# ScalarE's order in graph attention: the copy of the transposed probabilities ahead of the leaky ReLU in every slot

## The chip, the cores and the metric

The kernel runs on one core of one Trainium2 chip. The metric is the time of one execution on the device in microseconds (us), as a median over runs.

## What is computed

`x` holds 16 graphs of 1024 nodes with 256 features; `adj` holds their 1024 x 1024 adjacency matrices. One layer is graph attention with a residual, then a mixture of eight experts with a residual. The attention part, in which the change lies:

```python
h = _layernorm(x)
Wh = einsum('bnd,od->bno', h, W)
e = (Wh @ a1)[:, :, None] + (Wh @ a2)[:, None, :]
e = where(e > 0, e, 0.2 * e)          # leaky ReLU
e = where(adj == 0, -inf, e)
alpha = softmax(e, axis=-1)
x = x + einsum('bij,bjo->bio', alpha, Wh)
```

The second part applies to each row of the layer-normalised result, for each of eight experts, two matrix products with batch norm and ReLU and a third product, and adds them with weights of a softmax gate.

## The kernel before

The program has two blocks, one after the other: attention (to about 684 us) and the experts. Each engine has an instruction stream of its own, written out in a fixed order; engines meet through semaphores. The change is in ScalarE's stream of the attention block.

A batch (graph) is eight row tiles of 128 nodes. The block is a software pipeline of slots, one tile per slot: 16 slots `u` make a pair `k` of batches, and there are 8 pairs, with six slots ahead (`u` from -6). A tile `t` passes through several slots, at an offset from `u`:

- `t = u + 6`, VectorE: adjacency row and the row of the second score term give `scores` (L973).
- `t = u + 5`, ScalarE: `relu`, the leaky ReLU (Prelu) of the masked scores, in place (L789).
- `t = u + 4`, VectorE: `row_min` (L946), then ScalarE: `exponentials`, in place, with the row sum (L808). It signals `probs_ready`.
- `t = u + 3`, TensorE: 8 transposes `pT_ps<-ident,scores` (L681), which wait for `probs_ready`; ScalarE: `upper_half`, which copies `pT_ps` from PSUM to `pT_hi` in a shortened format (L799) and waits for those transposes (`pT_ready`); VectorE: the remainder `pT_lo` (L983).
- `t = u + 2`, TensorE: 24 matmuls `attn_ps` (L53 to L55), in the three products of upper and lower halves.
- `t = u + 1`, VectorE: normalise and add the residual (L956); ScalarE: negated mean (L839, every second slot) and sum of squares (L850).

So the tile that a slot's exponential finishes is the one that the next slot's transposes and copy take. TensorE's order in a slot is transposes, then any projection, then the 24 matmuls.

In four of the eight slots of a batch TensorE also projects the next batch's rows (call it head work; in the code `head and 1 <= head[1] <= HEADS`): four transposes of x (L638) at the end of the slot before, the projection (L655), ScalarE's copies `hT` (L757) and `wh_hi` (L766), VectorE's `wh_lo` (L925). The slot behind these four, with `head[1] == HEADS + 1`, opens on TensorE with eight transposes that spread a column over rows (L664), which ScalarE copies (`ej_rows`, L772); call it the row slot. In it, and in slot 10 of the last pair, the exponential stands ahead of the squares (`exp_first`). The row slot and the three behind it have no head work. The last batch has none in any slot, since no batch follows.

Of the kernel before, what the change touches and what calls it, by code (L numbers as in the profile page):

```python
# [282 lines left out]
def attention_block(nc, x, adj, W, a, W1, W2, x1_dram, ident, minus_half, ln_eps, w12_hi, w12_lo, feat_sum,  # L283
# [11 lines left out]
    HEADS = TB // 2  # L295
# [11 lines left out]
    with ctx:  # L307
# [65 lines left out]
        def tile_at(k, u, off, last):  # L373

            t = u + off
            ok = (t >= 0 or not isinstance(k, int)) and (t < UT or not last)
            return ok, t, k * UT + (t + 1)
# [18 lines left out]
        def task_at(k, i):  # L396

            return i // EP, k * EP + i % EP
# [21 lines left out]
        def parity(t):  # L420
            return (t // TB) % 2
# [330 lines left out]
        @block.scalar  # L752
        def _(act):
            def head_hT(b, j, first=False):
                xT, hT_j, _ = (first_head if first else later_head)(j)
                act.wait_ge(S["hT_psum"], b * HEADS + (j + 1))
                act.activation(hT_j.rearrange("p k c -> p (k c)"), xT, ACT.Copy) \  # L757
                    .then_inc(S["hT_ready"], 1)

            def head_wh(b, j, i, first=False):  # L760
                _, _, acc = (first_head if first else later_head)(j)
                act.wait_ge(S["xs_rstd_ready"], b * HEADS + (j + 1))
                for c in range(2):
                    t = 2 * j + c
                    act.wait_ge(S["wh_ready"], b * TB + (t + 1))
                    act.activation(wh_hi[i][:, t, :], acc[:, 1 - c, 0:D], ACT.Copy,  # L766
                                   scale=xs_rstd[:, j, 1 - c:2 - c]).then_inc(S["wh_hi_ready"], 1)

            def head_ej(b, i):
                act.wait_ge(S["ej_rows_psum"], 2 * b + 1)  # L770
                rows = (head_ps if b else attn_ps)[:, 0, :]
                act.activation(ej_rows[i][:, 0:BANK], rows, ACT.Copy, scale=-EDGE_UNIT) \  # L772
                    .then_inc(S["ej_left_ready"], 1)

            def split_weights_hi(k, i):

                layer, e = task_at(k, i)
                act.wait_ge(stage_in[i % 2], DMA * (k * EP + (i // 2 + 1)))
                act.activation(w12_hi[:, layer, e, :], w_stage[i % 2][:, :], ACT.Copy).then_inc(S["w12_hi_ready"], 1)

            def relu(k, u, last):

                ok, t, n = tile_at(k, u, 5, last)
                if ok:

                    act.wait_ge(S["masked_ready"], n)
                    if k == 0 and t < TB:
                        act.wait_ge(S["wh_lo_ready"], t // 2 * 2 + 2)
                    act.activation(scores[t % 4][:, 0:N], scores[t % 4][:, 0:N], ACT.Prelu, scale=SLOPE / EDGE_UNIT,  # L789
                                   bias=e_cols[parity(t)][:, (t % TB) ^ 1, 0:1], alpha=1.0 / SLOPE) \  # L790
                        .then_inc(S["lrelu_ready"], 1)

            def upper_half(k, u, last):

                ok, t, n = tile_at(k, u, 3, last)
                if ok:
                    act.wait_ge(S["pT_ready"], n)
                    wait(act, S["attn_ready"], n - 2)
                    act.activation(pT_hi[t % 2][:, :, :], pT_ps[t % 2][:, :, :], ACT.Copy) \  # L799
                        .then_inc(S["pT_hi_ready"], 1)  # L800

            def exponentials(k, u, last):

                ok, t, n = tile_at(k, u, 4, last)
                if ok:
                    c = slice(t % 4, t % 4 + 1)
                    act.wait_ge(S["min_ready"], n)
                    act.activation(scores[t % 4][:, 0:N], scores[t % 4][:, 0:N], ACT.Exp, scale=-1.0,  # L808
                                   bias=row_min[:, c], accum_out=row_sum[:, c]).then_inc(S["probs_ready"], 1)

            def slot(k, u, last):
                head = head_at(k, u, last)
                if head and 1 <= head[1] <= HEADS:
                    head_hT(2 * k + head[0], head[1] - 1)
                if head and head[1] == HEADS + 1:
                    head_ej(2 * k + head[0], head[0] % 2)
                if head and 1 <= head[1] <= HEADS:

                    upper_half(k, u, last)
                    relu(k, u, last)  # L820
                else:
                    relu(k, u, last)
                    upper_half(k, u, last)
                if head and 1 <= head[1] <= HEADS:
                    head_wh(2 * k + head[0], head[1] - 1, head[0] % 2)

                if last and u == GATE_SLOT + 2:
                    for d in range(KB):
                        act.wait_ge(first_tile.xT_psum, d + 1)
                        act.activation(first_tile.xT_hi[:, d, :], head_ps[:, d, :], ACT.Copy) \  # L830
                            .then_inc(first_tile.xT_hi_ready, 1)
                exp_first = (head and head[1] == HEADS + 1) or (last and u == NORM_SLOT + 1)
                if exp_first:
                    exponentials(k, u, last)

                post, pt, pn, pc = pair_at(k, u, 1, last)
                if post:
                    act.wait_ge(S["x1_ready"], k * UT + (pt + 1))
                    act.activation(x1_negmean[:, pc], x1_sum[:, pc], ACT.Copy, scale=-1.0 / D) \  # L839
                        .then_inc(S["x1_negmean_ready"], 1)  # L840
                squares = [pair_at(k, u, 1, last) + (-1,), pair_at(k, u, 0, last) + (0,)]
                if last and u == UT - 2:
                    squares[1] = pair_at(k, u + 1, 0, last) + (0,)
                if last and u == UT - 1:
                    squares = []
                for post, pt, pn, _, step in squares:
                    if post:
                        at = (pt + step) % 4
                        act.wait_ge(S["x1_negmean_ready"], pn)
                        act.activation(w_sb[:, at % 2, :], x1_sb[at][:, :], ACT.Square, bias=x1_negmean[:, at:at + 1],  # L850
                                       accum_out=x1_squares[:, at:at + 1]).then_inc(S["x1_squares_ready"], 1)
                if not exp_first:
                    exponentials(k, u, last)
                if u >= 0 and u % TASK_SLOTS == TASK_SLOTS // 2:
                    split_weights_hi(k, u // TASK_SLOTS)
                if last and u == GATE_SLOT + 1:
                    act.wait_ge(gates.featT_psum, 1)
                    act.activation(gate_featT, pT_ps[0][:, :, :].rearrange("p (t k) c -> p t (k c)", k=KB), ACT.Copy,
                                   scale=float(D) ** 0.5 / B).then_inc(gates.featT_ready, 1)
                    last_w.upper(act, 0)  # L860
                if last and u == GATE_SLOT + 2:
                    gates.exponentials(act)
                    act.wait_ge(gates.wT_psum, 1)
                    act.activation(first_tile.wT[0:E, :], pT_ps[0][0:E, CT:TB, :].rearrange("e t c -> e (t c)"),
                                   ACT.Copy).then_inc(gates.wT_ready, 1)

            head_hT(0, 0, first=True)
            head_hT(0, 1, first=True)
            act.wait_ge(S["ej_weights_psum"], 1)
            act.activation(ej_weights, attn_ps[:, 0, 0:D], ACT.Copy).then_inc(S["ej_weights_ready"], 1)  # L870
            act.wait_ge(S["wT_ready"], 1)
            act.activation(wx[:, :, :], head_ps[:, :, 0:DX], ACT.Copy).then_inc(S["wx_ready"], 1)
            head_hT(0, 2, first=True)
            head_hT(0, 3, first=True)
            head_ej(0, 0)
            for u in range(-6, 0):
                slot(0, u, PAIRS == 1)
                if -6 <= u < -6 + HEADS:
                    head_wh(0, u + 6, 0, first=True)
            for k in range(PAIRS - 1):  # L880
                for u in range(UT):
                    slot(k, u, False)
            for u in range(UT):
                slot(PAIRS - 1, u, True)
# [781 lines left out]
```

## Time and profile before

| | |
|---|---|
| median of 3 runs | 2808.19 us (2808.19 to 2808.91) |
| profiled execution, its own time | 2809.31 us |
| its span, first to last instruction | 2807.4 us |
| mean granted TensorE clock | 0.998 of full speed |
| TensorE (PE) busy | 2774.5 us, 99% |
| its weight loads (PEld) busy | 2469.6 us, 88% |
| VectorE (DVE) busy | 2413.1 us, 86% |
| ScalarE (ACT) busy | 2106.8 us, 75% |

A busy share is an average over the span. Matmuls are pipelined and overlap in the rows, so that a busy TensorE may still have room. What is to be read is which engine waits for which in a slot.

How the rows below are to be read. A row of the timeline: start in us, duration in us, engine, line, operation, output<-inputs, shapes, count of merged instructions, and in brackets the idle time ahead and what ended it. The next instruction of ScalarE starts some 0.1 us before the one ahead of it ends in the rows. A row of the windows: start and end, length, then busy us with instruction count for PE, PEld, DVE, ACT and POOL, then the granted clock, DMA share and GB/s. A row of the waits: engine and instruction, what it waited for, us in total, times, the longest.

### The profile page before, as it was taken

The numbers are of one execution on the slowest core, as the hardware profiler recorded it, in microseconds if no ns is written. First come the engines' busy times: TensorE is split into PE (matmuls) and PEld (weight loads), VectorE is DVE, ScalarE is ACT, GpSimd is POOL, SyncE is SP. The second block draws the span as 40 slices with busy tenths as digits, with TensorE's granted clock in tenths as the row PEclk, the third lists the DMA queues.
The fourth block names the chain that finished last, engine by engine and source line by source line (L and its number), as shares of the span: only waits on it lengthen the run. The fifth ranks groups of instructions, "written<-read, shape, count | busy, mean of one in ns | idle before, by whom it ended". The sixth has DMA issues, their size and how long they took to land.

```text
span 2807.4 us, 46140 instructions
## 1 busy us (share of the span) xinstructions
PE 2774.5 (99%) x17114; PEld 2469.6 (88%) x17114; DVE 2413.1 (86%) x3408; ACT 2106.8 (75%) x2832; POOL 487.5 (17%) x707
## 2 busy tenths in 40 slices
PE   8999999999999999999999999999999999999998
PEld 7999999998788888888888888888888888888887
DVE  8999999997888888888888888888888888888887
ACT  7889889887777777777777777777777777777775
POOL 4555555555000000000000000000000000001000
PEclk9999999999999999999999999999999999999999
DMA  4455555543455554545445455545545554545554
GB/s 163 154 167 163 157 166 162 162 153 119 139 170 165 161 166 154 165 156 161 163 155 165 154 165 161 165 153 170 157 163 157 160 164 154 166 154 163 153 162 145
DMA packets 160060, 445.91 MB, mean 159 GB/s; under 512 B 16032, under 2 KB 73800, under 8 KB 159840
## 3 DMA queue, kind: packets, MB, share of 16 engines
q1 hardware_dynamic: 159840, 442.98, 50.2%
q8 instruction: 138, 2.26, 0.3%
q14 instruction: 82, 0.67, 0.1%
HBM read 401.99 MB, written 40.93 MB: 158 GB/s over the span
## 4 chain that ended last, share of the span: by engine, by line
PE 74%; DVE 1%; ACT 0%; issue 0%; DMA 0%; DVEq 0%; ACTq 0%
PE head_ps L53 12%; PE head_ps L55 12%; PE head_ps L54 12%; PE m_ps L1284 7%; PE m_ps L1287 7%; PE m_ps L1286 7%; PE z_ps L55 4%; PE z_ps L53 4%; PE z_ps L54 4%; PE turn_ps L1257 1%; PE turn_ps L1265 1%; DVE h_lo L1569 0%; DVE h_sums L1576 0%; DMA wo_ops<-wo_scratch 0%; ACT h_hi L1432 0%
## 5 line engine op out<-in xcount | busy, mean ns | idle before, releaser
L1416 ACT ACTIVATE h<-head_ps,bn_shift,bn_scale 128x512 f32<-128x512 f32 x768 | 593.9, 774 | 532.5 <-PE head_ps L55 319.9
L1569 DVE TENSOR_TENSOR h_lo<-h_sums,h_hi 128x1792 fp32r<-128x1792 f32 (+1 forms) x257 | 518.2, 2017 | 199.9 <-ACT h_hi L1432 199.8
L1432 ACT ACTIVATE h_hi<-h_sums 128x1792 fp32r<-128x1792 f32 (+1 forms) x257 | 435.4, 1694 | 63.6 <-DVE h_sums L1589 58.0
L1576 DVE TENSOR_TENSOR h_sums<-h,gate_row 128x1024 f32<-128x1024 f32 x256 | 313.7, 1225 | 114.5 <-ACT h L1416 96.7
L87 POOL TENSOR_TENSOR ffn_vareps<-ffn_mv,ln_eps 128x4 f32<-128x4 f32 x32 | 7.1, 223 | 1860.4 <-DVE ffn_mv L81 1860.4
L1536 DVE TENSOR_TENSOR h_lo<-h,h_hi 128x1024 fp32r<-128x1024 f32 x256 | 311.9, 1218 | 6.8 <-ACT h_hi L1446 6.8
L53 PE MATMUL attn_ps<-wh_hi,pT_hi 128*128 128x256 f32 x1024 | 304.9, 298 | 0.0
L54 PE MATMUL attn_ps<-wh_lo,pT_hi 128*128 128x256 f32 x1024 | 287.9, 281 | 0.0
L55 PE MATMUL attn_ps<-wh_hi,pT_lo 128*128 128x256 f32 x1024 | 287.8, 281 | 0.0
L1446 ACT ACTIVATE h_hi<-h 128x1024 fp32r<-128x1024 f32 x256 | 270.9, 1058 | 0.1
L1284 PE MATMUL m_ps<-h_hi,wo_ops 128*128 128x256 f32 x896 | 256.0, 286 | 3.1 <-DMA wo_ops<-wo_scratch 3.1
L1284 PE MATMUL m_ps<-h_hi,wh_lo 128*128 128x256 f32 x896 | 256.4, 286 | 0.0
L1286 PE MATMUL m_ps<-h_lo,wh_lo 128*128 128x256 f32 x896 | 250.4, 279 | 0.0
L1286 PE MATMUL m_ps<-h_lo,wo_ops 128*128 128x256 f32 x896 | 250.2, 279 | 0.0
L1287 PE MATMUL m_ps<-h_hi,wh_lo 128*128 128x256 f32 x896 | 250.0, 279 | 0.0
L1287 PE MATMUL m_ps<-h_hi,wo_ops 128*128 128x256 f32 x896 | 249.9, 279 | 0.0
L53 PE MATMUL head_ps<-wh_hi,w_hi 128*128 128x512 f32 x512 | 203.9, 398 | 3.8 <-ACT h L1416 3.3
L55 PE MATMUL head_ps<-wh_hi,w_lo 128*128 128x512 f32 x512 | 203.2, 397 | 0.0
L54 PE MATMUL head_ps<-wh_hi,w_hi 128*128 128x512 f32 x512 | 202.7, 396 | 0.0
L53 PE MATMUL head_ps<-xT_hi,w_hi 128*128 128x512 f32 x512 | 202.7, 396 | 0.0
L55 PE MATMUL head_ps<-h_hi,w_lo 128*128 128x512 f32 x512 | 201.5, 394 | 0.0
L53 PE MATMUL z_ps<-h_hi,w_hi 128*128 128x512 f32 x512 | 200.8, 392 | 0.4 <-DVE h_lo L1536 0.4
(215 smaller groups left out, 7619.3 us busy)
## 6 DMA issues: line engine op xcount, KB each, us to landing
wh_lo<-wo_scratch SPq DMA_DIRECT2D x124, 896.0 KB, 6.4
wo_ops<-wo_scratch SPq DMA_DIRECT2D x124, 896.0 KB, 6.5
adj_sb<-in_adj SPq DMA_DIRECT2D x128, 512.0 KB, 3.5
gate_row<-w_scratch SPq DMA_DIRECT2D x256, 256.0 KB, 4.6
x_sb<-in_x SPq DMA_DIRECT2D x64, 256.0 KB, 2.9
x_scratch<-x_sb SPq DMA_DIRECT2D x128, 128.0 KB, 1.8
ffn_x<-x_scratch SPq DMA_DIRECT2D x16, 512.0 KB, 7.6
x_sb<-x_scratch SPq DMA_DIRECT2D x16, 512.0 KB, 7.5
```

Of the source, the lines that this page charges most:

```text
L53: pe.matmul(out, w_hi, x_hi, start=first, stop=False)
L54: pe.matmul(out, w_hi, x_lo, start=False, stop=False)
L55: return pe.matmul(out, w_lo, x_hi, start=False, stop=last)
L1284: pe.matmul(m_at(q), w_hi, x_hi[:, x, :], start=e == 0 and q in OPENERS, stop=False, skip_group_check=True)
L1286: pe.matmul(m_at(q), w_hi, x_lo[:, x, :], start=False, stop=False, skip_group_check=True)
L1287: done = pe.matmul(m_at(q), w_lo, x_hi[:, x, :], start=False, stop=e == E - 1, skip_group_check=True)
L1416: return act.activation(dst, src, ACT.Relu, bias=bn_shift[layer][:, col], scale=bn_scale[layer][:, col])
L1432: act.activation(h2_hi[s % 2][:, a:b, :], g2[:, 1 + a:1 + b, :], ACT.Copy) \
L1446: act.activation(h1_hi[s % 2][:, :, :], h1[:, :, :], ACT.Copy).then_inc(S["h1_hi_ready"], 1)
L1536: dve.tensor_tensor(h1_lo[s % 2][:, :, :], h1[:, :, :], bits(h1_hi[s % 2][:, :, :]), ALU.subtract) \
L1569: dve.tensor_tensor(h2_lo[s % 2][:, a:b, :], g2[:, 1 + a:1 + b, :], bits(h2_hi[s % 2][:, a:b, :]), ALU.subtract).then_inc(S["h2_lo_ready"], 1)
L1576: dve.tensor_tensor(h2_rows, h2[:, :, :], gate[s % 2][:, :].unsqueeze(1).to_broadcast([P, KB, BANK]), ALU.mult).then_inc(S["gated_ready"], 1)
```

## The change

In slots with head work ScalarE already issues the copy of the transposed probabilities (`upper_half`) ahead of the leaky ReLU (`relu`). In the others the leaky ReLU came first. Now the copy comes first in all. No instruction is added or removed, and the other engines' streams are as they were.

```diff
-                if head and 1 <= head[1] <= HEADS:
-
-                    upper_half(k, u, last)
-                    relu(k, u, last)
-                else:
-                    relu(k, u, last)
-                    upper_half(k, u, last)
+                upper_half(k, u, last)
+                relu(k, u, last)
```

Sixty-six slots have both instructions and no head work: slot -3, then slots 2 to 5 and 10 to 13 of each of the first seven pairs (56), then slots 2 to 10 of the last pair (9).

ScalarE's stream in a row slot and the first slot behind it, before (`scores<-scores,e_cols` is the leaky ReLU, `pT_hi<-pT_ps` the copy, `scores,row_sum<-scores,row_min` the exponential):

```order
L772 ACTIVATE ej_rows<-head_ps 128x512 [waits ej_rows_psum]
L789 ACTIVATE scores<-scores,e_cols 128x1024 [waits masked_ready]
L799 ACTIVATE pT_hi<-pT_ps 128x1024 [waits attn_ready,pT_ready]
L808 ACTIVATE scores,row_sum<-scores,row_min 128x1024 [waits min_ready]
L839 ACTIVATE x_negmean<-x_sum 128x2 [waits x1_ready]
L850 ACTIVATE w_sb,x_squares<-x_sb,x_negmean 128x256 [waits x1_negmean_ready]
L789 ACTIVATE scores<-scores,e_cols 128x1024 [waits masked_ready]
L799 ACTIVATE pT_hi<-pT_ps 128x1024 [waits attn_ready,pT_ready]
```

The same place of the changed kernel (five lines fewer in the file, so L845 is L850 of before, and L834 is L839):

```order
L772 ACTIVATE ej_rows<-head_ps 128x512 [waits ej_rows_psum]
L799 ACTIVATE pT_hi<-pT_ps 128x1024 [waits attn_ready,pT_ready]
L789 ACTIVATE scores<-scores,e_cols 128x1024 [waits masked_ready]
L808 ACTIVATE scores,row_sum<-scores,row_min 128x1024 [waits min_ready]
L834 ACTIVATE x_negmean<-x_sum 128x2 [waits x1_ready]
L845 ACTIVATE w_sb,x_squares<-x_sb,x_negmean 128x256 [waits x1_negmean_ready]
L799 ACTIVATE pT_hi<-pT_ps 128x1024 [waits attn_ready,pT_ready]
L789 ACTIVATE scores<-scores,e_cols 128x1024 [waits masked_ready]
```

The two instructions have changed places in each slot; nothing else moved. In the last pair, slots 7 and 8 (no head work in any slot there), ScalarE's stream reads in the changed kernel:

```order
L799 ACTIVATE pT_hi<-pT_ps 128x1024 [waits attn_ready,pT_ready]
L789 ACTIVATE scores<-scores,e_cols 128x1024 [waits masked_ready]
L845 ACTIVATE w_sb,x_squares<-x_sb,x_negmean 128x256 [waits x1_negmean_ready]
L808 ACTIVATE scores,row_sum<-scores,row_min 128x1024 [waits min_ready]
L799 ACTIVATE pT_hi<-pT_ps 128x1024 [waits attn_ready,pT_ready]
L789 ACTIVATE scores<-scores,e_cols 128x1024 [waits masked_ready]
L834 ACTIVATE x_negmean<-x_sum 128x2 [waits x1_ready]
L845 ACTIVATE w_sb,x_squares<-x_sb,x_negmean 128x256 [waits x1_negmean_ready]
L808 ACTIVATE scores,row_sum<-scores,row_min 128x1024 [waits min_ready]
```

Here, too, the copy now stands directly behind the exponential of the slot before, with the leaky ReLU behind it.

TensorE's stream at the start of a slot without head work is the same before and after; it shows what the transposes wait for:

```order
L681 MATMUL pT_ps<-ident,scores 128x128 [waits pT_lo_ready,probs_ready]
L681 MATMUL pT_ps<-ident,scores 128x128 x7
L53 MATMUL attn_ps<-wh_hi,pT_hi 128x256 [waits x1_ready,pT_lo_ready]
L54 MATMUL attn_ps<-wh_lo,pT_hi 128x256
L55 MATMUL attn_ps<-wh_hi,pT_lo 128x256
```

Nothing moved on this engine.

## Rows read from the trace of the kernel before

**Rows 1.** The page, busy time of each engine.

```profile
PE 2774.5 (99%) x17114; PEld 2469.6 (88%) x17114; DVE 2413.1 (86%) x3408; ACT 2106.8 (75%) x2832; POOL 487.5 (17%) x707
```

**Rows 2.** Windows: four slots without head work, then four with it.

```profile
178.30:194.41 16.11, 15.85 (x135) 15.45 (x134) 15.70 (x26) 15.70 (x28) 10.31 (x15) 1.00 0.59 182
194.41:218.93 24.52, 24.52 (x183) 23.20 (x182) 23.04 (x48) 20.70 (x39) 12.50 (x20) 1.00 0.47 151
```

**Rows 3.** Waits of TensorE's weight loads, 60 to 660 us.

```profile
PEld pT_ps L681 <- ACT scores L808: 12.7, 34, 0.6
PEld head_ps L638 <- DVE wh_lo L925: 4.2, 12, 0.9
```

**Rows 4.** Timeline of TensorE: the transposes that open eight slots.

```profile
178.30 1.04 PE L681 MATMUL pT_ps<-ident,scores 128*128 128x128 f32 x8
...
182.05 1.03 PE L681 MATMUL pT_ps<-ident,scores 128*128 128x128 f32 x8
...
186.09 1.09 PE L681 MATMUL pT_ps<-ident,scores 128*128 128x128 f32 x8
...
190.16 1.09 PE L681 MATMUL pT_ps<-ident,scores 128*128 128x128 f32 x8
...
194.41 1.04 PE L681 MATMUL pT_ps<-ident,scores 128*128 128x128 f32 x8
...
200.37 1.04 PE L681 MATMUL pT_ps<-ident,scores 128*128 128x128 f32 x8
...
206.55 1.04 PE L681 MATMUL pT_ps<-ident,scores 128*128 128x128 f32 x8
...
218.93 1.04 PE L681 MATMUL pT_ps<-ident,scores 128*128 128x128 f32 x8
```

**Rows 5.** Timeline of ScalarE in the slots without head work.

```profile
178.56 1.14 ACT L789 ACTIVATE scores<-scores,e_cols 128x1024 f32<-128x1024 f32 x1
179.60 1.02 ACT L799 ACTIVATE pT_hi<-pT_ps 128x1024 fp32r<-128x1024 f32 x1
180.50 1.15 ACT L808 ACTIVATE scores<-scores,row_min 128x1024 f32<-128x1024 f32 x1
...
183.42 1.00 ACT L799 ACTIVATE pT_hi<-pT_ps 128x1024 fp32r<-128x1024 f32 x1
...
184.81 1.14 ACT L808 ACTIVATE scores<-scores,row_min 128x1024 f32<-128x1024 f32 x1
185.85 0.19 ACT L808 ACTIVATION_READ_ACCUMULATOR scores<-scores,row_min 128x1 f32 x1
185.94 1.14 ACT L789 ACTIVATE scores<-scores,e_cols 128x1024 f32<-128x1024 f32 x1
187.22 1.03 ACT L799 ACTIVATE pT_hi<-pT_ps 128x1024 fp32r<-128x1024 f32 x1
...
188.88 1.14 ACT L808 ACTIVATE scores<-scores,row_min 128x1024 f32<-128x1024 f32 x1
```

**Rows 6.** Timeline of TensorE: two openings in early head work.

```profile
77.72 1.04 PE L681 MATMUL pT_ps<-ident,scores 128*128 128x128 f32 x8
...
84.49 1.04 PE L681 MATMUL pT_ps<-ident,scores 128*128 128x128 f32 x8
```

**Rows 7.** Timeline of TensorE: two openings in the last batch.

```profile
626.36 1.04 PE L681 MATMUL pT_ps<-ident,scores 128*128 128x128 f32 x8
...
662.44 1.03 PE L681 MATMUL pT_ps<-ident,scores 128*128 128x128 f32 x8
```

**Rows 8.** Timeline of TensorE near the start.

```profile
26.98 1.09 PE L681 MATMUL pT_ps<-ident,scores 128*128 128x128 f32 x8 [1.80 <-ACT scores L808]
28.20 3.69 PE L655 MATMUL head_ps<-wx,hT 128*128 128x258 f32 x8
```

**Rows 9.** Windows: granted clock in two short stretches.

```profile
29.00:31.00 2.00, 2.00 (x6) 1.52 (x6) 2.00 (x4) 1.65 (x3) 0.00 (x0) 0.50 0.28 113
698.00:700.00 2.00, 1.13 (x5) 0.60 (x5) 0.00 (x0) 1.52 (x2) 0.40 (x2) 1.00 0.01 4
```

## The prediction

> **What bounds the kernel now.** I read the page first, for the bound: TensorE is busy 99% of the span [rows 1]. Then the windows of one batch in the middle of attention, for the two kinds of slot. The four slots with head work take 24.52 us and TensorE has 24.52 us of busy rows in them; the four without take 16.11 us, with 15.85 us [rows 2]. ScalarE has 15.70 us in those same 16.11 us, so there it is nearly as full as TensorE; in the other four it has 20.70 of 24.52 us. Then the waits: in 600 us of attention TensorE's weight loads for the transposes waited 12.7 us for the exponential, 34 times, and those of the head work 4.2 us for VectorE's `wh_lo` [rows 3]. Last the timeline, for who hands over to whom in a slot.
>
> The reader is to see one thing there. TensorE's transposes at 186.09 start when the exponential's sum is out (185.85 + 0.19 = 186.04) [rows 4, 5]. ScalarE's copy of their result starts at 187.22, 1.13 us after they began. What ScalarE does in between is the leaky ReLU, 185.94 to 187.08 [rows 5]. The transposes of a slot and ScalarE's leaky ReLU lie side by side, and both are about as long.
>
> **The change, part by part.** No instruction is added or dropped, so no engine's work changes. What changes is the order of two instructions of ScalarE in 66 slots. ScalarE runs its stream in order: with the copy in front, it waits behind the exponential until the slot's transposes are done, and the leaky ReLU, squares and the next exponential are queued behind it. TensorE's next transposes wait for that exponential. So the slot becomes a closed chain: exponential, transposes, copy, leaky ReLU, squares, exponential. The change puts no other work under the transposes.
>
> Its length, from rows. Exponential start to the transposes that it releases: 184.81 to 186.09, 1.28 us. Transposes to copy: 1.13 us (186.09 to 187.22). Copy start to exponential start: 183.42 to 184.81, 1.39 us with the squares between; 187.22 to 188.88, 1.66 us where the negated mean is there as well, every second slot; 179.60 to 180.50, 0.90 us in the row slot, where the exponential follows directly. The leaky ReLU now lies in this stretch as well: 1.04 us (178.56 to 179.60) [rows 4, 5]. From opening to opening that gives:
> - row slot: 1.13 + 0.90 + 1.04 + 1.28 = 4.35 us
> - plain slot: 1.13 + 1.39 + 1.04 + 1.28 = 4.84 us
> - slot with the negated mean: 1.13 + 1.66 + 1.04 + 1.28 = 5.11 us
>
> A batch has one row slot, two plain ones and one with the mean: 4.35 + 4.84 + 5.11 + 4.84 = 19.14 us. Today the same four openings span 178.30 to 194.41, 16.11 us [rows 4]. The loss is 3.03 us. TensorE alone needs 3.75 us for such a slot (178.30 to 182.05, no wait), so it isn't hidden there: TensorE will stand idle 0.6 to 1.4 us in each. The squares of the row slot and the weight copy (`w12_hi`, L779) of another, which come after an exponential, fall into the new wait and cost nothing; the cover is the 1.13 us of transposes. Mean and squares take 1.66 - 0.90 = 0.76 us [rows 5]; the weight copy has half the copy's columns (512 against 1024), so it is below its 1.03 us. Without that cover the two would add 0.76 and up to 1.03 us a batch. The first 14 batches with such slots: 14 x 3.03 = 42.4 us.
>
> The last batch has no head work. Its row slot opens at 626.36 and slot 11 at 662.44, 36.08 us for nine openings [rows 7]. By the chain these are one row slot, four plain, three with the mean, and slot 10, where the exponential again follows directly: 4.35 + 4 x 4.84 + 3 x 5.11 + 4.35 = 43.39 us. The loss is 7.3 us. Behind slot 10 there is no leaky ReLU left, and the end of the block moves as a whole.
>
> Slot -3, in the filling of the pipeline: at most one leaky ReLU, 1.04 us, at least nothing, as TensorE waits there for other things too (1.80 us at 26.98) [rows 8]. I take the middle, 0.5 us.
>
> Can it be regained in the slots with head work? Their order isn't touched, and TensorE goes from opening to opening without a wait (5.96 us, 194.41 to 200.37), save for the one wait on `wh_lo`: 6.18 us for the next (200.37 to 206.55) [rows 4], and 6.77 us in the first such batch (77.72 to 84.49) [rows 6]. That wait is there because VectorE lags. It gains 3 us a batch to catch up, and needs `wh_lo` 0.2 us earlier. So 0.2 us x 14 and the 0.8 us of the first come back, together some 3.7 us; the waits say 4.2 us over this stretch [rows 3]. I take 4, of 0 to 5.
>
> Adding up: 42.4 + 7.3 + 0.5 - 4 = 46.2 us. The profiled execution took 2809.31 us (its span is 2807.4, with 1.9 us around it), which gives 2855.5 us; the median of the runs is 1.1 us lower, so 2854 us, 1.6% slower.
>
> Is the 99% real? Here the weight loads are the check: 23.20 us of the 24.52 us with head work, 95% [rows 2]. [...] By that 1.32 us of each such stretch would be slack, and the sum would be near 32 us; by the openings, that come 5.96 us apart with no wait, it is 46 us. I go by the openings.
>
> **The rivals.**
>
> (a) *Hidden slack.* TensorE's stretch with head work gives back what the weight loads leave free, 24.52 - 23.20 = 1.32 us in 14 batches, 18 us instead of my 4: 46.2 - 14.5 = 32 us, 2840 us. Against it: these slots show next to no wait, and nothing in their streams gets shorter. 4%.
>
> (b) *The clock falls.* Near the start, behind 1.80 us of idle, TensorE's granted clock was 0.50 (29 to 31 us), its lower level of 1.2 GHz, and eight projection matmuls took 3.69 us, half of it, 1.85 us, being the price [rows 8, 9]. In 698 to 700 us it was idle for 0.87 of 2 us and the clock stayed at 1.00 [rows 9]. My new gaps, up to 1.4 us, lie between the two. Should it fall once a batch, 15 x 1.85 = 28 us are added: 2882 us. For it: the gaps come again each slot. Against: 3.7 us of dense matmuls lie between any two. 5%. The Trainium skill (TensorE: Matmul & The Clock Gate, A second HAM failure mode: psum-queue depth-cycling) tells of a kernel whose frequent short idles between groups of matmuls made the clock swing; no row here has it in steady slots.
>
> (c) *Faster.* The copy is ready earlier, so `pT_lo` is too, VectorE loses its lag, and the wait on `wh_lo` (4.2 us) goes, while the leaky ReLU proves not to be late for anyone. The time would be 2808 - 4 = 2804 us. It would need the transposes of a slot not to wait for the exponential just ahead; the start at 186.09, 0.05 us behind it, says that they do. It decides for this side if that exponential ends no later than today. 2%.
>
> (d) *No effect.* The copy finds its transposes already done, because TensorE is ahead; then the order of two ready instructions is free: 2808 us. It holds in no slot whose exponential is the last arrival. Even in the row slot the transposes only open at 178.30, 0.3 us ahead of the leaky ReLU's start [rows 4, 5]. 2%.
>
> **How the numbers follow.** My sum has 87%. Its own bounds: with 5 us regained, nothing in slot -3 and 0.07 us less for the handover in each of 66 slots (as ScalarE, idle, may start sooner), 40 us, 2848; with nothing regained, 1.04 in slot -3 and 0.1 us more per slot, 57 us, 2865. A little of (a) below: 2844 to 2867 holds 8 in 10. Within 0.2%, 5.6 us, a measurement of this kernel can't tell a difference. Slower by more: the sum, (a) and (b), 96%; same 2%; faster 2%.
>
> **What the changed profile would show.** Openings in slots without head work 4.35, 4.84, 5.11, 4.84 us apart; the idle of `pT_hi` L799 behind the transposes on ScalarE near 1.1 us in each, and of the transposes L681 behind `scores` L808 some 0.6 to 1.4 us; slots with head work as before, all near 6.0 us, without waits on `wh_lo`; VectorE's waits moved to `pT_lo` behind the copy; clock 1.00 in the middle of attention; the experts' block as long as before. The prediction is wrong if the openings stay near 4.1 us, or if the slots with head work fall under 5.9 us, or if the granted clock falls in attention.

## The result and the profile after

The changed kernel takes 2853.87 us (median of 3 runs, 2853.72 to 2856.07) against 2808.19 us: a ratio of 1.0166, with a 95% interval of 1.0148 to 1.0184. It is 45.7 us slower; 2854 us were forecast. The profiled execution took 2856.07 us, with a span of 2854.1 us, and was the slowest of the three.

The page after the change, which answers to [rows 1]:

```profile
PE 2777.9 (97%) x17114; PEld 2470.8 (87%) x17114; DVE 2435.6 (85%) x3408; ACT 2110.2 (74%) x2832; POOL 481.0 (17%) x707
```

The busy time of the engines is about what it was; TensorE has 3.4 us more in a span 46.7 us longer, and VectorE 22.5 us more, of which the last section tells. What grew most is idle time. The windows of one batch, first the four slots without head work, then the four with it [rows 2]:

```profile
185.76:204.91 19.15, 16.23 (x134) 15.39 (x132) 18.55 (x29) 16.08 (x29) 10.04 (x16) 1.00 0.55 160
204.91:229.20 24.29, 24.29 (x180) 23.22 (x181) 21.98 (x45) 20.54 (x39) 12.37 (x19) 1.00 0.46 146
```

The first stretch is 19.15 us long instead of 16.11, with 16.23 us of TensorE in it: it is now idle for 2.92 us, and ScalarE for 3.07 us. Both wait in turns. The second is still full of TensorE, and a little shorter (24.29 us against 24.52). The granted clock is 1.00 in both. The waits of TensorE's weight loads from 60 to 700 us [rows 3]:

```profile
PEld pT_ps L681 <- ACT scores L808: 61.5, 62, 1.4
```

12.7 us have become 61.5 us, and the row of `wh_lo` is gone. On ScalarE, a slot of the changed kernel in the timeline [rows 5]:

```profile
193.66 1.14 ACT L808 ACTIVATE scores<-scores,row_min 128x1024 f32<-128x1024 f32 x1
194.70 0.19 ACT L808 ACTIVATION_READ_ACCUMULATOR scores<-scores,row_min 128x1 f32 x1
196.07 1.03 ACT L799 ACTIVATE pT_hi<-pT_ps 128x1024 fp32r<-128x1024 f32 x1 [1.18 <-PE pT_ps L681]
197.00 1.14 ACT L789 ACTIVATE scores<-scores,e_cols 128x1024 f32<-128x1024 f32 x1
198.04 0.19 ACT L834 ACTIVATE x_negmean<-x_sum 128x2 f32<-128x2 f32 x1
198.26 0.51 ACT L845 ACTIVATE w_sb<-x_sb,x_negmean 128x256 f32<-128x256 f32 x1
...
198.77 1.13 ACT L808 ACTIVATE scores<-scores,row_min 128x1024 f32<-128x1024 f32 x1
```

The exponential's sum is out at 194.89 us. The transposes open at 194.94. The copy starts at 196.07 after 1.18 us of idle, and the leaky ReLU, the mean, the squares and the next exponential follow. The transposes in the timeline of TensorE [rows 4]:

```profile
185.76 1.04 PE L681 MATMUL pT_ps<-ident,scores 128*128 128x128 f32 x8
...
190.08 1.09 PE L681 MATMUL pT_ps<-ident,scores 128*128 128x128 f32 x8 [0.41 <-ACT scores L808]
...
194.94 1.09 PE L681 MATMUL pT_ps<-ident,scores 128*128 128x128 f32 x8 [0.90 <-ACT scores L808]
...
200.05 1.09 PE L681 MATMUL pT_ps<-ident,scores 128*128 128x128 f32 x8 [1.15 <-ACT scores L808]
...
204.91 1.09 PE L681 MATMUL pT_ps<-ident,scores 128*128 128x128 f32 x8 [0.47 <-ACT scores L808]
...
210.85 1.04 PE L681 MATMUL pT_ps<-ident,scores 128*128 128x128 f32 x8
...
216.82 1.04 PE L681 MATMUL pT_ps<-ident,scores 128*128 128x128 f32 x8
...
229.20 1.04 PE L681 MATMUL pT_ps<-ident,scores 128*128 128x128 f32 x8
```

Openings are 4.32, 4.86, 5.11 and 4.86 us apart, where 3.75, 4.04, 4.07 and 4.25 stood, and each but the first shows its wait for the exponential. The last batch, in two openings [rows 7], takes 43.47 us instead of 36.08:

```profile
664.37 1.04 PE L681 MATMUL pT_ps<-ident,scores 128*128 128x128 f32 x8
...
707.84 1.09 PE L681 MATMUL pT_ps<-ident,scores 128*128 128x128 f32 x8 [0.41 <-ACT scores L808]
```

Adding the openings up over the block gives an account that the experiments below use as well. "Without" and "with" are the stretches without and with head work, summed over the 14 batches that have both; "last" is from the last batch's row slot to its slot 11.

| us | first row slot at | without | with | last |
|---|---|---|---|---|
| before | 54.42 | 225.6 | 346.3 | 36.1 |
| changed | 55.10 | 268.2 | 341.0 | 43.5 |
| e1, copy first in row slots alone | 54.14 | 236.9 | 344.1 | 36.7 |
| e7, copy first only ahead of head work | 54.28 | 234.3 | 342.2 | 36.3 |
| e2, copy first, squares behind | 54.36 | 245.6 | 346.8 | 39.3 |
| e5, copy first, half a leaky ReLU | 52.84 | 244.3 | 342.0 | 39.6 |
| e3, leaky ReLU first, squares behind | 53.74 | 223.2 | 354.8 | 35.4 |
| e4, leaky ReLU first in every slot | 54.84 | 225.4 | 346.3 | 36.1 |
| e6, before with half a leaky ReLU | 52.26 | 221.1 | 350.6 | 36.6 |
| e8, before with thin GpSimd | 54.53 | 225.1 | 344.6 | 35.6 |
| e9, before with `wh_lo` earlier | 52.39 | 225.2 | 342.4 | 36.0 |
| e10, e3 with `wh_lo` earlier | 52.30 | 223.2 | 344.0 | 35.4 |
| e11, changed with `wh_lo` earlier | 54.63 | 268.2 | 341.1 | 43.5 |

From before to changed: 42.6 us lost without head work, 5.3 us regained with it, 7.4 us lost in the last batch. The first row slot comes 0.7 us later, but that is a sum of three things. Slot -3 opens 1.73 us later (25.00 us against 23.27), with no edited instruction ahead of it; it lasts 4.35 us instead of 3.71, which is the edit; and behind the next transposes the kernel before lost some 1.7 us to a fall of the clock [rows 8, 9] that the changed one did not have (6.47 us to the following opening against 8.16). Such starts and falls, which the edits do not give, are most of the 2.8 us by which the kernels differ in this column.

### The profile page after: what moved, and what is told of

Read it like the earlier page. It is cut to its first block, busy times and chain, and to the rows that moved or that the text cites. A ratio compares the mean times of both kernels' runs of the same rounds, so it can differ in the third digit from the quotient of the medians.

```text
span 2854.1 us, 46140 instructions
## 1 busy us (share of the span) xinstructions
PE 2777.9 (97%) x17114; PEld 2470.8 (87%) x17114; DVE 2435.6 (85%) x3408; ACT 2110.2 (74%) x2832; POOL 481.0 (17%) x707
## 4 chain that ended last, share of the span: by engine, by line
PE 73%; DVE 1%; ACT 0%; issue 0%; DMA 0%; DVEq 0%; ACTq 0%
PE head_ps L53 12%; PE head_ps L55 12%; PE head_ps L54 12%; PE m_ps L1279 7%; PE m_ps L1282 7%; PE m_ps L1281 7%; PE z_ps L55 4%; PE z_ps L53 4%; PE z_ps L54 4%; PE turn_ps L1252 1%; PE turn_ps L1260 1%; DVE h_lo L1564 0%; DVE h_sums L1571 0%; DMA wo_ops<-wo_scratch 0%; ACT h_hi L1427 0%
## 5 line engine op out<-in xcount | busy, mean ns | idle before, releaser
L55 PE MATMUL z_ps<-h_hi,w_lo 128*128 128x512 f32 x512 | 201.1, 393 | 0.0
```

The source lines that it names most:

```text
L55: return pe.matmul(out, w_lo, x_hi, start=False, stop=last)
```

## The experiments

The kernel before was run beside each. Its medians were 2809.57 us for e1 to e4, 2809.23 us for e5 to e8, 2808.72 us for e9 and e10, and 2809.29 us for e11.

### e1: the copy first in the row slots alone

```diff
-                if head and 1 <= head[1] <= HEADS:
+                if head and 1 <= head[1] <= HEADS + 1:
```

> The order is changed in the 15 row slots alone; the other slots are as before. Theory (closed chain, and ScalarE nearly as full as TensorE behind it): the row slot lasts 4.32 us as in the changed kernel, against 3.75; ScalarE's exponential comes 0.83 us later there and ScalarE, with 15.70 us of work in the 16.11 us of such slots, cannot catch up before the head work, so 0.83 us a batch are lost, not 0.57: 15 x 0.83 = 12.5 us less some 3 us regained from the wait on wh_lo, 2817.5 us; the slot behind the row slot shows 4.3 us instead of 4.04. Rival (each slot pays for itself): 15 x 0.57 less 3 us, and the next slots swallow even that in the waits they had: at most 2814 us.

This is an edit of the kernel before. Measured: 2819.53 us, ratio 1.0035 (1.0022 to 1.0049), 10.0 us slower. TensorE's openings in the timeline:

```profile
180.02 1.04 PE L681 MATMUL pT_ps<-ident,scores 128*128 128x128 f32 x8
184.34 1.09 PE L681 MATMUL pT_ps<-ident,scores 128*128 128x128 f32 x8 [0.41 <-ACT scores L808]
188.65 1.09 PE L681 MATMUL pT_ps<-ident,scores 128*128 128x128 f32 x8 [0.34 <-ACT scores L808]
192.71 1.09 PE L681 MATMUL pT_ps<-ident,scores 128*128 128x128 f32 x8
```

The row slot is 4.32 us long and the next one 4.31 instead of 4.04, so the delay is 0.57 + 0.27 = 0.84 us and not 0.57 (the table has 11.3 us for 14 batches, 0.81 each). The unchanged slot behind pays too, since ScalarE has no room to catch up. The rival is out: a slot doesn't pay for itself alone.

### e2: the copy first, with the squares behind the exponential

```diff
-                exp_first = (head and head[1] == HEADS + 1) or (last and u == NORM_SLOT + 1)
+                exp_first = not (head and 1 <= head[1] <= HEADS) or (last and u == NORM_SLOT + 1)
```

> Copy in front of the leaky ReLU in every slot, and in slots without head work the negated mean and the squares moved behind the exponential. Theory (closed chain): they fall under the transposes that ScalarE waits for, so each such slot lasts as long as the row slot, 4.32 to 4.35 us, 4.45 where the weight copy is there too: about 17.45 us for four, 1.3 more than before, and 39.2 us for the nine openings of the last batch; 14 x 1.35 + 3.1 + 0.7 - 4 = 18.7 us, 2827 us. Rival (the cost is the hand-over to a copy that waits, whatever else is in the slot): 2854 us as the changed kernel, since ScalarE's idle of about 1.1 us a slot stays.

This is an edit of the changed kernel. Measured: 2836.17 us, ratio 1.0095 (1.0081 to 1.0109). The rival (2854 us) is wrong: moving work under the transposes took 19 us off the changed kernel. The slots came out as the chain has them, 245.6 us for 14 batches, 17.5 each, and 39.3 us for the last. But 8 us more were lost than I had said. More than half of that is in the stretches with head work: they took 346.8 us and regained nothing, where 4 us were expected. Another 1.1 us is in the slots without, and 2.4 us lie behind slot 11 of the last batch. VectorE's waits show something that no other kernel here has at this size:

```profile
DVE row_inv L937 <- POOL row_den L555: 18.4, 17, 1.7
```

It waited 18.4 us for GpSimd's `row_den`. In GpSimd's timeline that operation (the second row) stands behind the one that needs the squares (the first), with the large operations on the normalised rows between them:

```profile
192.68 0.20 POOL L560 TENSOR_TENSOR x_vareps<-x_squares,sum_eps 128x2 f32<-128x2 f32 x1 [6.71 <-ACT w_sb L845]
...
196.72 0.21 POOL L555 TENSOR_TENSOR row_den<-row_sum,tiny 128x2 f32<-128x2 f32 x1
```

Late squares hold GpSimd, GpSimd holds the row sums, and VectorE keeps its lag. That is read from the rows and was not tried by itself. e5 is the nearest comparison, with slots as short and the squares in their place. Late squares alone do not make the wait: e3 and e10 have them too, and VectorE waited 1.4 us for `row_den` there.

### e3: the order of before, with the squares behind the exponential

The edit of e2 on the kernel before.

> The order of before (leaky ReLU first without head work), with the negated mean and the squares behind the exponential in those slots. Theory: the exponential comes 0.5 us earlier in its slot, so the transposes' waits on it (0.35 and 0.32 us a batch) go; ScalarE, with 15.7 us of work in four such slots, becomes the bound of them: up to 0.4 us a batch and 1 us in the last, 2802 to 2806 us. Rival (TensorE bound, the waits are made up by VectorE's lag): 2808 us, no change.

Measured: 2815.96 us, ratio 1.0023 (1.0014 to 1.0033), 6.4 us slower where 2802 to 2806 us, a gain, had been expected. TensorE's waits:

```profile
PEld head_ps L638 <- DVE wh_lo L925: 11.3, 15, 0.8
PEld attn_ps L53 <- DVE pT_lo L983: 7.9, 17, 0.7
PEld pT_ps L681 <- ACT scores L808: 1.8, 2, 1.4
```

The wait on the exponential is gone, as expected, from 12.7 us to 1.8. The slots without head work got 2.4 us shorter in all. Then TensorE waited for `wh_lo` and `pT_lo`, and the stretches with head work got 8.5 us longer. VectorE has no room. From its first mask of a row slot to its `wh_lo` of the third slot with head work it is busy without a gap, and it already was in the kernel before (window from 138.65 us):

```profile
138.65:169.10 30.45, 30.07 (x233) 28.65 (x232) 30.45 (x57) 27.62 (x50) 19.57 (x28) 1.00 0.55 168
```

In e3 it is 30.85 of 30.86 us. TensorE opening earlier only meets a VectorE that is no earlier. So before the change three engines were nearly level in these slots, not two.

### e4: the leaky ReLU first in every slot

```diff
-                if head and 1 <= head[1] <= HEADS:
-
-                    upper_half(k, u, last)
-                    relu(k, u, last)
-                else:
-                    relu(k, u, last)
-                    upper_half(k, u, last)
+                relu(k, u, last)
+                upper_half(k, u, last)
```

> The opposite of the change: leaky ReLU in front of the copy in every slot, those with head work too. Theory: with head work ScalarE has 20.70 us of work in 24.52 us, and its copy waits only 0.27 us for the transposes; the leaky ReLU fills that, the copy comes 0.77 us later and the exponential no later than before, so TensorE loses nothing: 2806 to 2811 us. Rival (the copy's place matters by how early pT_lo is ready): VectorE falls behind by 0.77 us in each of 60 such slots and wh_lo makes TensorE wait, up to 0.8 us x 15 = 12 us, 2820 us.

Measured: 2809.58 us against 2809.57, ratio 1.0002 (0.9993 to 1.0011). The rival's 12 us are out. With head work the order of the two makes no difference: there ScalarE has room, and waits for TensorE at `hT` already, ahead of both (32.5 us in 55 waits of the kernel before, from 60 to 684 us).

### e5 and e6: half a leaky ReLU, with the copy first and with it second

```diff
-                    act.activation(scores[t % 4][:, 0:N], scores[t % 4][:, 0:N], ACT.Prelu, scale=SLOPE / EDGE_UNIT,
+                    act.activation(scores[t % 4][:, 0:BANK], scores[t % 4][:, 0:BANK], ACT.Prelu, scale=SLOPE / EDGE_UNIT,
```

> The changed kernel with the leaky ReLU applied to the first 512 of the 1024 scores only (the others stay without it), so that it takes some 0.6 us less 0.1 instead of 1.04. Theory (the leaky ReLU now lies in the closed chain): each of the 66 slots gets shorter by the whole 0.43 us as long as it stays over TensorE's 3.75 us: openings 3.9, 4.44, 4.67, 4.44 us; 2855.3 - 28 = 2827 us on this chip, and somewhat more if VectorE, which then has less time to catch up, keeps a wait on wh_lo. Rival (ScalarE's work is not in the chain, the hand-over is): under 5 us gained.

> The kernel before with the same halved leaky ReLU. Theory (here VectorE is as full as ScalarE, and the transposes' waits are small change): the waits on the exponential go, and waits on pT_lo and wh_lo come in their place: 2806 to 2812 us. Rival (ScalarE is the bound of the slots without head work): 4 x 0.43 us a batch, of which TensorE can take 0.67: 10 us, 2800 us.

e5 is an edit of the changed kernel, e6 of the kernel before; both leave the second half of the scores without a leaky ReLU. Measured: e5 2826.08 us, ratio 1.0059 (1.0045 to 1.0074), 29 us less than the changed kernel's 46 us above before would give (2855). e6 2808.66 us, ratio 1.0000 (0.9991 to 1.0010). The same 0.43 us cut from the same instruction is worth 29 us where the copy stands first, and nothing where it stands second. TensorE's waits in e5, then in e6:

```profile
PEld pT_ps L681 <- ACT scores L808: 35.9, 64, 1.0
PEld head_ps L638 <- DVE wh_lo L920: 0.8, 1, 0.8
```

```profile
PEld head_ps L638 <- DVE wh_lo L925: 8.9, 15, 0.8
PEld pT_ps L681 <- ACT scores L808: 6.7, 18, 0.6
```

In e5 the openings are 3.89, 4.44, 4.68 and 4.44 us apart, each 0.42 or 0.43 less than in the changed kernel. In e6 the waits on the exponential halved (12.7 us before) and those on `wh_lo` doubled (4.2 us before), as in e3; the wait on `pT_lo` that had been expected beside them did not come. And e5 regained 4.4 us with head work (346.3 to 342.0) where e2, with slots of the same length, did not: what differs is where the squares stand and the half leaky ReLU, and with them VectorE's wait for `row_den`, 18.4 us in e2 and 0.4 us in e5.

### e7: the copy first only in the slot ahead of the head work

```diff
-                if head and 1 <= head[1] <= HEADS:
+                if (head and 1 <= head[1] <= HEADS) or (u % TB == 5 and u > 0):
```

> The order is changed only in the slot right ahead of the head work (15 slots). Theory: the transposes of the next slot wait for the later exponential, 0.6 us (a weight copy covers part of ScalarE's wait here), and then the head work's slack on ScalarE takes up the rest, so 0.6 us a batch and no more: 15 x 0.6 = 9 us less up to 4 regained from the wait on wh_lo, 2815 to 2819 us; the opening of the first slot with head work comes 4.85 us after the last. Rival (a leaky ReLU is lost each time, wherever it is): 15 x 1.04 = 16 us, 2825 us.

Measured: 2813.64 us, ratio 1.0016 (1.0007 to 1.0025), 4.4 us slower, just under my bounds. The slot is 4.87 us long instead of 4.25, so 8.7 us are lost in 14 batches, the 0.62 us each that were expected. The stretches with head work gave back 4.1 of the 5.3 us of the changed kernel. TensorE's waits:

```profile
PEld pT_ps L681 <- ACT scores L808: 22.7, 47, 1.1
PEld head_ps L638 <- DVE wh_lo L925: 1.0, 2, 0.7
```

The wait on `wh_lo` fell from 4.2 us to 1.0: 0.6 us of delay right ahead of the head work is enough for VectorE to catch up, in all batches but the first.

### e8: GpSimd's large operations cut to 8 columns

```diff
-                pool.tensor_tensor(rows, rows, n1_sb[t // 2 % 2][:, :, :], ALU.add).then_inc(S["n1_added"], 1)
+                pool.tensor_tensor(rows[:, :, 0:8], rows[:, :, 0:8], n1_sb[t // 2 % 2][:, :, 0:8], ALU.add).then_inc(S["n1_added"], 1)
...
-                        pool.tensor_scalar(n1_sb[t // 2 % 2][:, i, :], x1_sb[at][:, :], x1_negmean[:, at:at + 1],
+                        pool.tensor_scalar(n1_sb[t // 2 % 2][:, i, 0:8], x1_sb[at][:, 0:8], x1_negmean[:, at:at + 1],
```

> The kernel before with GpSimd's two large operations on the normalised rows (L541 and L570) cut to 8 of 256 columns, so that the feature sums are not computed. Theory (VectorE's lag costs the kernel before the waits on wh_lo, and part of that lag is VectorE's operations lasting longer beside GpSimd's): VectorE's masking (L973) falls from a mean of 1253 ns to 1210, the waits on wh_lo shrink, and 2 to 5 us are gained, 2805 to 2807 us. Rival (the waits have another cause): no change, 2809.6 us.

Measured: 2805.22 us, ratio 0.9985 (0.9976 to 0.9994). VectorE's masking, in the groups by line from 100 to 600 us (busy us, mean ns), and TensorE's wait on `wh_lo`:

```profile
L973 DVE SCALAR_TENSOR_TENSOR scores<-adj_sb,ej_rows 128x1024 f32<-128x1024 int32 x99 | 120.8, 1220 | 2.9 <-PE pT_ps L681 2.9
```

```profile
PEld head_ps L638 <- DVE wh_lo L925: 2.0, 8, 0.7
```

The mean fell from 1253 to 1220 ns and the wait from 4.2 to 2.0 us. VectorE's lag was what TensorE waited for, and GpSimd is part of the lag. By the table the gain is 0.5 us without head work, 1.7 with it and 0.5 in the last batch; the rest of the 4.0 us between the medians lies outside those slots, and no row ties it to the edit.

### e9: `wh_lo` earlier, in the kernel before

```diff
-                if head and step == 1:
-                    head_wh(hb, 0, hi)
+                if head and step in (1, 2):
+                    head_wh(hb, step - 1, hi)
...
-                if head and 2 <= step <= HEADS:
+                if head and 3 <= step <= HEADS:
```

> The kernel before, with VectorE's wh_lo of the second slot with head work in front of pT_lo and the aggregation, as it already stands in the first. Nothing is left out. Theory (the wait of the next transposes of x on wh_lo, 0.2 us a batch and up to 0.8 in some, is pure TensorE idle, which the changed kernel got back by the way): wh_lo is ready 1.1 us earlier, the third opening comes 5.97 us after the second, not 6.18; 4 us less than before, 2805 to 2806 us. Rival (pT_lo, now 0.9 us later, takes the place of the wait): no change or slower, 2809 to 2812 us.

Measured: 2804.37 us, ratio 0.9985 (0.9976 to 0.9993), 4.4 us faster than before. It computes everything and beats both kernels. (The forecast held 0.2% for the least difference that can be told; with 10 runs or more of each the intervals are 0.1% to either side, so 0.15% is clear of noise.) TensorE's waits:

```profile
PEld pT_ps L681 <- ACT scores L808: 12.3, 34, 0.6
PEld head_ps L638 <- DVE wh_lo L925: 0.9, 1, 0.9
```

The wait on `wh_lo` went from 4.2 us to 0.9, that on the exponential stayed, and the stretches with head work fell from 346.3 to 342.4 us. One more microsecond was gained where the pipeline fills, ahead of the first row slot: the wait on `wh_lo` from 20 to 60 us fell from 1.4 us to 0.4.

### e10: `wh_lo` earlier and squares behind, leaky ReLU first

The edits of e3 and e9 together.

> The same edit on the kernel with leaky ReLU first and the squares behind the exponential (2816 us, whose waits were 11.3 us on wh_lo and 7.9 us on pT_lo). Theory (VectorE was its bound from the row slot to the second slot with head work, and an order that serves wh_lo first takes the wait from where it is longest): 5 to 8 us less, 2808 to 2811 us, the waits on pT_lo staying. Rival (VectorE is busy throughout, so the wait only moves to pT_lo): 2816 us.

Measured: 2804.41 us, ratio 0.9987 (0.9978 to 0.9996). That is 11.5 us less than e3 (10.7 with each against its own kernel before), more than the 5 to 8 us expected, and the same as e9. TensorE's waits:

```profile
PEld attn_ps L53 <- DVE pT_lo L983: 7.9, 17, 0.7
PEld head_ps L638 <- DVE wh_lo L925: 0.7, 1, 0.7
```

11.3 us on `wh_lo` became 0.7, and the 7.9 us on `pT_lo` stayed. So the two were not the same delay counted in two places. In all it is no better than e9: it is ahead of it at slot 11 of the last batch (654.87 us against 656.03) and 1.3 us behind it at the first matmuls of the experts' block (`m_ps<-ident,node_table`), 677.28 us against 675.99. Two things lie between, in the profiled executions:

```profile
670.66 0.50 PE L53 MATMUL head_ps<-wh_hi,w_hi 128*128 128x512 f32 x1 [1.66 <-DVE wh_hi L1000]
670.60:675.10 4.50, 4.44 (x12) 3.29 (x13) 2.87 (x12) 0.62 (x3) 3.77 (x5) 0.62 0.00 0
```

TensorE waited 1.66 us for VectorE's `wh_hi` where e9 has 0.42 us, and the matmuls behind it ran at a mean granted clock of 0.62 and took 4.45 us where e9's took 2.90 at 1.00.

### e11: `wh_lo` earlier, in the changed kernel

The edit of e9 on the changed kernel.

> The changed kernel with wh_lo of the second slot with head work ahead of pT_lo, the edit that took 4.4 us off the kernel before. Theory (the changed kernel has no wait on wh_lo left, having got that back already): no change from the changed kernel, 45 to 47 us over the kernel before, 2854 to 2856 us. Rival (the edit helps by itself, and the changed kernel regained nothing): 4 us less, 2850 us.

Measured: 2853.04 us, ratio 1.0155 (1.0138 to 1.0172), 43.8 us above before; the span of the profiled execution is 2854.0 us against the changed kernel's 2854.1. TensorE's waits:

```profile
PEld pT_ps L681 <- ACT scores L808: 61.5, 62, 1.4
```

They are those of the changed kernel to the tenth. The median lies between theory (45 to 47 us) and rival (some 41). From the first row slot on nothing was gained, as the openings are the same. But the theory, that no wait on `wh_lo` is left, overlooked the filling of the pipeline. From 20 to 60 us, the changed kernel and then e11:

```profile
PEld head_ps L638 <- DVE wh_lo L920: 1.4, 2, 1.0
```

```profile
PEld head_ps L638 <- DVE wh_lo L920: 0.4, 1, 0.4
```

There e11 gained 1.0 us. Its span does not show it, since after the transposes near the start it took 8.12 us to the next opening, with a granted clock of 0.51 from 30 to 33 us, where the changed kernel took 6.47 at 1.00. So from the first row slot on the gain of e9 and what the changed kernel regained are one and the same thing; the 1.0 us ahead of it is e9's and e11's alone.

## Why the prediction was right

**The chain.** Forecast: openings 4.35, 4.84, 5.11 and 4.84 us apart; measured: 4.32, 4.86, 5.11, 4.86. That the leaky ReLU had become a link of it was argued from rows; e5 shows it (29 us for 0.43 us in 66 slots, which would be 28; by the openings 27.8 us of it lie in the slots), and e6 shows that it was none before. That the squares are a link as well, e2 shows. One sign was put too simply: ScalarE's idle ahead of the copy is 1.18 us only where nothing else lies behind the exponential. Where the row slot's squares, the weight copy or `hT` do, it is 0.45, 0.66 and 0.70 us, the cover that the forecast's own sum allowed for.

**The cover that was lost.** The forecast put it down to the transposes and the leaky ReLU lying side by side. e5 and e6 bear it out: the leaky ReLU's length counts where it lies behind the copy, and not where it lies beside the transposes. e4 shows that the copy's place as such has no price: with head work, where ScalarE has 3.8 us a batch to spare [rows 2], the order is free.

**The sum.** 14 batches: 42.4 us forecast, 42.6 measured. Last batch: 7.3 and 7.4. Slot -3: 0.5, the middle of a range, and 0.64 (from its opening to the next). Regained: 4, measured 5.3. Together 46.2 us forecast and 45.3 measured in the slots; the medians differ by 45.7. That the medians come so near is in part luck. In the profiled executions, whose spans differ by 46.7 us, the other 1.4 us come from outside the edited slots and are a balance of larger things: the later start (+1.7 us), falls of the clock, of which the kernel before has two (-1.7 and -1.5) and the changed one has one (+1.5), and 1.4 us more of which no row here shows the cause. So the experts' block, forecast to be as long as before, took 2.4 us longer from its first matmuls (`m_ps<-ident,node_table`) on, and the way there from slot 11 was 1.0 us shorter.

**What was regained, and why.** The step "VectorE lags and gains 3 us a batch to catch up" is shown by e7 (0.6 us is enough), e9 and e11, and e8 agrees. The size was low, 4 us against 5.3: in the first batch with head work the first slot gave back 0.87 us and the second 0.74, where the forecast had 0.8 for both, and in the other 13 batches they gave back 0.03 and 0.25 us each, where it had nothing and 0.2. "All near 6.0 us" holds for three slots with head work; the fourth takes 6.4 us in both kernels. After the change VectorE waits for others in its place:

```profile
DVE pT_lo L978 <- ACT pT_hi L799: 16.0, 31, 1.0
DVE wh_lo L920 <- ACT wh_hi L766: 14.8, 40, 0.8
```

That VectorE was so nearly a third bound I had not seen. It does no harm to the forecast, as a longer slot gives it time; it is what made e3 fail.

**The rivals.** Hidden slack: the stretches with head work gave back 5.3 us and not 18, and 4.2 of that was the wait on `wh_lo`. The share of weight loads in them (23.20 of 24.52 us) was no measure of room. The clock: 1.00 from 60 to 722 us, with gaps of 0.6 to 1.4 us (5.11 less 3.75) in every slot without head work, so it does not fall there. Faster: every slot without head work got longer. No effect: e4 has that case, in the slots with head work.

## What to carry to other kernels

When an engine waits for a result that its own last output sets off on another engine (here exponential, transposes, copy), look for what stands in its stream between the two. That work is free as long as it is there; moved behind the wait, its length went into the cycle here (0.43 us less of it made each slot 0.43 us shorter in e5). A nearly full engine does not catch up: e1's single slot made the next one longer too. Before taking a wait away, look who is level with the bound: with three engines within a few per cent, the first edit (e3) only handed the wait on and lost 6 us, while serving the late consumer first (e9) gained 4.

## What the runs showed of the hardware that was not expected

VectorE's masking, which reads two tensors from SBUF, lasts 1.22 us alone. In the changed kernel it lasted 2.25 us (2.23 to 2.25) in 12 of 93 cases, each beside GpSimd's split of the weights, which also reads two from SBUF. VectorE, then GpSimd, in the timeline:

```profile
200.72 2.25 DVE L968 SCALAR_TENSOR_TENSOR scores<-adj_sb,ej_rows 128x1024 f32<-128x1024 int32 x1
```

```profile
200.59 1.29 POOL L547 TENSOR_TENSOR w_lo<-w_stage,w_hi 128x512 fp32r<-128x512 f32 x1 [0.96 <-ACT w_hi L779]
```

The mask started 0.13 us behind GpSimd's operation and lasted 1.03 us longer. In e5, where the two overlap by some 0.74 us instead of 1.17, it lasted 1.8 us in 11 cases. Beside GpSimd's sum and normalisation of rows (L541, L570) it lasted 1.65 us, in 12 more. In the kernel before mask and split overlapped by 0.2 us at most: the mean there is 1253 ns, in the changed one 1448. The Trainium skill (GPSIMD Engine Reference, Specifications) says that GpSimd shares its SBUF interfaces with VectorE and contends with VectorE's instructions that have two SBUF inputs; the rows agree. No wait of TensorE on VectorE is left in the changed kernel from 60 us on, so it cost nothing there. That the overlap is the cause was not tried by itself; in e8, where GpSimd's sum and normalisation are thin, no mask took more than 1.27 us.

The clock near the start: behind 1.80 us of idle in the kernel before, eight projection matmuls took 3.69 us at a granted clock of 0.50 [rows 8, 9]. Behind 2.44 us of idle at the same place the changed kernel's took 2.01 us, at full clock:

```profile
29.35 1.09 PE L681 MATMUL pT_ps<-ident,scores 128*128 128x128 f32 x8 [2.44 <-ACT scores L808]
30.56 2.01 PE L655 MATMUL head_ps<-wx,hT 128*128 128x258 f32 x8
```

The changed kernel's clock fell at the start of the experts' block instead, behind 1.99 us of idle (0.53 is the mean of the second window):

```profile
726.00:728.00 2.00, 0.12 (x1) 0.15 (x2) 0.00 (x0) 0.66 (x2) 1.45 (x2) 1.00 0.04 8
728.00:730.00 2.00, 2.00 (x10) 1.91 (x10) 0.33 (x1) 1.97 (x3) 0.00 (x0) 0.53 0.29 90
```

In e9 the same place has 1.99 us of idle too, and the clock stays:

```profile
675.99:677.99 2.00, 2.00 (x13) 1.83 (x14) 0.90 (x1) 1.97 (x3) 0.00 (x0) 1.00 0.33 65
```

And at the end of attention it fell in the kernel before behind 0.43 us of idle, and not in the changed one behind 0.44. The stretch with the same twelve matmuls, before and then changed:

```profile
676.90:681.30 4.40, 4.39 (x12) 3.43 (x13) 2.82 (x11) 0.57 (x3) 3.72 (x5) 0.62 0.00 0
```

```profile
722.40:725.30 2.90, 2.90 (x13) 2.25 (x14) 2.73 (x11) 0.55 (x3) 2.32 (x3) 1.00 0.00 0
```

So the length of the gap just ahead does not tell whether the clock falls. Each fall cost some 1.5 to 1.7 us, and a difference of a few microseconds between two profiled executions can be made of them.
